# A four-layer FFN kernel on one core: its convolution kernel built in two halves, a fourth adapter buffer, and small steps of layers 2 and 3 in other places

## The reference

```
x = x + L0_ffn(L0_cond(x))   # long convolution along the features, masked; then a 512x512 FP8 weight
x = x + L1_ffn(L1_cond(x))   # one of 16 adapter matrices (512x512) per sequence; then SwiGLU, NF4 weights, hidden 1376
x = x + L2_ffn(L2_cond(x))   # 512x512 base + top-2 gated rank-16 experts; then 128 slots, top 8, uncertainty gate
x = x + L3_ffn(L3_cond(x))   # masked mean over features, 5-tap filter over tokens, sigmoid gate; 512x512 + rank-32 mix
```

## Time and profile before

| | us |
|---|---|
| median of 3 timed runs | 953.33 |
| lowest, highest | 950.3, 957.39 |
| the profiled execution, its own time | 951.24 |
| its span, first to last instruction | 949.5 |
| TensorE busy | 885.1 (93%) |
| VectorE busy | 579.8 (61%) |
| ScalarE busy | 390.1 (41%) |
| GpSimd busy | 86.9 (9%) |

### The profile page before, as it was taken

One profiled execution on the slowest core, in us unless ns is written; L12 is line 12 of the kernel. 1 busy time (PEld: TensorE's weight loads), 2 busy tenths in 40 slices (PEclk: granted clock), 3 DMA queues, 4 the chain that ended last, 5 costly groups with the idle time before them and its releaser, 6 DMA issues.

```text
span 949.5 us, 10316 instructions
## 1 busy us (share of the span) xinstructions
PE 885.1 (93%) x3261; PEld 474.5 (50%) x3262; DVE 579.8 (61%) x880; ACT 390.1 (41%) x458; POOL 86.9 (9%) x127
## 2 busy tenths in 40 slices
PE   0299998999999999999999999999989999899998
PEld 0296448998444444444444444444434555354442
DVE  7889977886998888888997300000132354158444
ACT  2024637876777776676687100000012132241200
POOL 5100009600000000000000000002201011100000
PEclk9999998999999999999999999999999999999999
DMA  6873127562000000000000300024010000002022
GB/s 203 317 242 134 74 81 246 195 223 70 23 22 23 17 31 0 31 30 1 30 1 0 87 13 1 0 72 136 1 45 1 1 1 1 1 1 44 0 89 88
DMA packets 32967, 61.19 MB, mean 64 GB/s; under 512 B 5880, under 2 KB 8264, under 8 KB 31704
## 3 DMA queue, kind: packets, MB, share of 16 engines
q1 hardware_dynamic: 32216, 60.50, 18.8%
q0 software_dynamic: 704, 0.10, 0.3%
HBM read 51.07 MB, written 8.47 MB: 63 GB/s over the span
## 4 chain that ended last, share of the span: by engine, by line
PE 83%; DVE 12%; issue 2%; DMA 1%; ACT 1%; POOLq 1%; POOL 0%; SPq 0%; ACTq 0%; DVEq 0%
PE ps L820 81%; DVE acc L1374 2%; DVE T L1374 2%; PE ps L861 1%; DVE W2T L1218 1%; PE ps L1075 1%; DVE W2T L1224 1%; POOLq L603 1%; DVE W2T L1221 1%; DVE raw L1352 0%; DVE amax L1345 0%; DMA T<-kpad 0%; DVE W1T L1218 0%; DVE Up L1551 0%; DVE Yp L1659 0%
## 5 line engine op out<-in xcount | busy, mean ns | idle before, releaser
L652 ACT ACTIVATE above<-raw,cst 128x1024 bf16<-128x1024 f32 (+2 forms) x225 | 271.8, 1231 | 122.1 <-DVE acc L1374 46.5
L820 PE MATMUL ps<-Yp,W3T 128*128 (+2 forms) x872 | 183.9, 367 | 6.6 <-POOL Yp L605 2.6
L1374 DVE SCALAR_TENSOR_TENSOR acc<-above,acc 128x1024 f32<-128x1024 bf16 (+2 forms) x112 | 148.1, 1323 | 18.3 <-ACT above L652 11.6
L820 PE MATMUL ps<-Up,W1T 128*128 128x512 f32 x344 | 155.5, 594 | 3.0 <-DVE Up L1473 1.9
L820 PE MATMUL ps<-Up,W2T 128*128 128x512 f32 (+1 forms) x392 | 155.1, 593 | 0.0
L820 PEld LDWEIGHTS ps<-Yp,W3T 128*128 128x128 f32 (+1 forms) x872 | 121.9, 196 | 63.7 <-issue 61.5
L1374 DVE SCALAR_TENSOR_TENSOR T<-above,T 128x1024 f32<-128x1024 bf16 (+1 forms) x84 | 114.1, 1359 | 20.9 <-ACT above L652 18.0
L820 PE MATMUL ps<-X,W3T 128*128 128x512 f32 (+1 forms) x256 | 113.7, 602 | 0.6 <-DVE Yp L1659 0.6
L820 PEld LDWEIGHTS ps<-Up,W2T 128*128 128x128 f32 (+1 forms) x392 | 64.2, 177 | 83.0 <-issue 83.0
L820 PEld LDWEIGHTS ps<-Up,W1T 128*128 128x128 f32 x344 | 64.1, 190 | 82.5 <-issue 76.3
L1495 DVE TENSOR_TENSOR X<-X,Yp x16 | 4.6, 349 | 125.6 <-issue 125.6
(11 more groups left out here) (299 smaller groups left out, 753.4 us busy)
## 6 DMA issues: line engine op xcount, KB each, us to landing
W3T<-in_wa SPq DMA_DIRECT2D x11, 1024.0 KB, 6.3
raw<-in_w SPq DMA_DIRECT2D x20, 256.0 KB, 3.3
W3T<-kpad SPq DMA_DIRECT2D x9, 512.0 KB, 5.0
Up<-in_xconv SPq DMA_DIRECT2D x4, 1024.0 KB, 11.5
X<-in_xT SPq DMA_DIRECT2D x1, 4096.0 KB, 22.9
xkeep<-X SPq DMA_DIRECT2D x4, 1024.0 KB, 4.5
X<-xkeep SPq DMA_DIRECT2D x4, 1024.0 KB, 9.6
W3T<-in_wa SPq DMA_DIRECT2D x5, 768.0 KB, 4.6
```

What stands on the lines that cost most here:

```text
L652: nc.scalar.activation(above[0:h, m % 2, 0:w], raw[0:h, u % 2, 0:w], ACT.Relu, scale=STEEP, bias=cst[0:h, C_BND + i:C_BND + i + 1]).then_i ...
L820: return nc.tensor.matmul(o, l, r, start=start, stop=stop, **kw)
L1374: V.scalar_tensor_tensor(out=ac, in0=src, scalar=float(STEPS[i]), in1=ac, op0=ALU.min, op1=ALU.add).then_inc(s["m_used"], 1)
```

## The change

- The convolution kernel is made in two halves of 16 heads: phases, sine, factors, matmuls and skip term each run twice with half the columns, into banks 6 and 7. The store to DRAM is four pieces per half. TensorE makes the second half after convolution group 1 (`make_k(1)`), and VectorE does `skip_term(1)` after `start_unit(0)`, ahead of the sort chain. SP stores the second half after strip 4.
- VectorE dequantises the FP8 weight after `conv_out(3)`; SP waits for that (`d_w0`) after issuing strip 8, then loads weight unit 1 and a quarter of X. X is loaded in quarters of 1 MB: two early, one after strip 8, one after strip 12.
- NCV, NF0, NAD become 4, 28, 54 instead of 10, 26, 50.
- Four adapter buffers: adapters 0 to 2 are loaded at the end of the convolution, 3 when the FFN ends, 4 right after; `keep(3)` and the load of unit 3 come behind adapter 4. GX and GA become 3; GpSimd copies the two further sequences. Unit 1 is transposed after the FFN, and copied by ScalarE after its three sequence copies.
- `prepare_values()`, the second part of `prepare()`, runs after the last down product.
- The four variance transposes of a block go to banks 3, 2, 5, 3.
- `slices(0)` is split in two and runs inside the last block of layer 2, one part before and one behind the wait for its `p_c2` inputs.
- Gates are spread in pairs: odd blocks lie in partitions 0 to 63, even ones in 64 to 127; a pair is two matmuls of 64 rows into banks 0 and 1. The memset of zeros on GpSimd goes.

```diff
-GX = 4
-GA = 4
+GX = 3
+GA = 3
...
-        NCV, NF0, NAD = 10, 26, 50
+        NCV, NF0, NAD = 4, 28, 54
@@ SP
             load_unit(0)
-            sp.dma_start(X[:, :, :], A["xT"].rearrange("(c p) n -> p c n", p=P)).then_inc(s["l_x"], 16)
+            load_x(0)
+            load_x(1)
...
-            sp.wait_ge(s["d_k"], 1)
-            for q in range(4):
-                sp.dma_start(kr[:, q * HQ:(q + 1) * HQ, :], ksb[q * 32:q * 32 + LA, :, :]).then_inc(s[f"l_kp{q}"], 16)
+            store_k(0)
...
                 if g == NS - 1:
+                    store_k(1)
+                if g == HG // 2:
                     sp.wait_ge(s["d_w0"], 1)
                     load_unit(1)
 
+                if g in (8, 12):
+                    load_x((8, 12).index(g) + 2)
...
             sp.wait_ge(s["p_conv"], HG)
-            load_adapter(0)
-            load_adapter(1)
+            sp.wait_ge(s["d_w0"], 1)
+            for a in range(NWS - 1):
+                load_adapter(a)
...
-            for a in range(2, ADAPT):
-                if a == 2:
+            for a in range(NWS - 1, ADAPT):
+                if a == NWS - 1:
                     sp.wait_ge(s["d_ord"], 1)
                     sp.wait_ge(s["p_ffn0"], TB * DC)
-                if a >= NWS:
-                    done = sp.value_load(order[0:1, NB + a - 2:NB + a - 1], min_val=0, max_val=NGR)
+                else:
+                    done = sp.value_load(order[0:1, NB + a - NWS + 1:NB + a - NWS + 2], min_val=0, max_val=NGR)
...
                 load_adapter(a)
-                if a == 2:
+                if a == NWS:
                     keep(TB - 1)
                     for u in units_between(K_FFN0[(TB - 1) * DC - 1], K_FFN0[-1]):
                         load_unit(u + 2)
@@ TensorE
                 last.then_inc(s["p_conv"], 1)
+                if g == 1:
+                    make_k(1)
...
                 for u in turns_ffn0(n):
-                    turn_unit(u)
+                    if u == 0:
+                        turn_unit(u)
...
+            turn_unit(1)
             pe.wait_ge(s["ad_out"], NG)
...
+            prepare_values()
             pe.wait_ge(s["d_x2"], NB // 2)
             pe.wait_ge(s["g_x2"], NB // 2)
...
                 if tb + 1 < TB:
                     logits(tb + 1)
+                else:
+                    pe.wait_ge(s["a_ha"], TB)
+                    slices(0, range(0, 2))
                 pe.wait_ge(s["d_hg"], tb + 1)
...
                     rank_in(tb + 1)
                     turn_logits(tb + 1)
+                else:
+                    slices(0, range(2, DC))
                 pe.wait_ge(s["a_c2"], tb + 1)
...
-                    if tb or t >= 2:
-                        pe.wait_ge(s["d_st"], NT * tb + t - 1)
-                    else:
-                        pe.wait_ge(s["a_va"], 1)
+                    if t == 0:
+                        pe.wait_ge(s["d_st"], NT * tb) if tb else pe.wait_ge(s["a_va"], 1)
+                    if t == 3:
+                        pe.wait_ge(s["d_st"], NT * tb + 1)
...
-                mm(ps[:, tb % 2, :], ones[:, :], gex[tb], True, True).then_inc(s["p_gb"], 1)
+                for k, half in ((0, slice(YM, P)), (1, slice(0, YM))):
+                    mm(ps[:, k, :], ones[half, :], gex[tb + k], True, True).then_inc(s["p_gb"], 1)
@@ VectorE
+            factors(0)
+            angles(1)
+            skip_term(0)
+            whole_turns(1)
...
+            factors(1)
...
             start_unit(0)
-            dve.wait_ge(s["l_w0"], 32)
-            link(V.tensor_copy(h16a, w0u))
...
+            skip_term(1)
             dve.wait_ge(s["p_ord"], 1)
...
                 conv_out(g)
-            dve.wait_ge(s["l_x"], 16)
+                if g == 3:
+                    dequantise_w0()
+                    dve.wait_ge(s["d_w0"], 1)
+            dve.wait_ge(s["l_x"], 16 * DC)
```

More of the change, by code:

```diff
@@ L286, in build @@
         mx2, gm2 = w2f[:, 4928:4930], w2f[:, 4932:4934]
-        gex = [w3f[:, i * TW:(i + 1) * TW] for i in range(TB)]
+        gex = [w3f[(0 if i % 2 else YM):(YM if i % 2 else P), i // 2 * TW:(i // 2 + 1) * TW] for i in range(TB)]
         wT = w3f[0:E, 2048:3072]
@@ L596, in _ @@
             g0 = GX + GA
-            first = [pool.value_load(order[0:1, g0 + i:g0 + i + 1], min_val=0, max_val=NB - 1) for i in range(12)]
+            first = [pool.value_load(order[0:1, g0 + i:g0 + i + 1], min_val=0, max_val=NB - 1) for i in range(14)]
             pool.wait_ge(s["d_x1"], TB * DC)
@@ L679, in _ @@
                                ).then_inc(s["a_xs"], 1)
+            evac_quant(1)
             for a in range(ADAPT):
@@ L820, in mm, with make_k @@
                 return nc.tensor.matmul(o, l, r, start=start, stop=stop, **kw)
-            pe.wait_ge(s["d_pp"], 1)
-            pe.wait_ge(s["d_kz"], 1)
-            for i in range(HQ):
-                for q in range(4):
-                    h = q * HQ + i
-                    last = mm(ps[q * 32:q * 32 + LA, 6, i * LC:(i + 1) * LC], pc[:, h, :], trig[:, h, 0:LC], True, True)
-            last.then_inc(s["p_k"], 1)
+            pe.wait_ge(s["d_kz"], 2)
+            def make_k(f):
+                pe.wait_ge(s["d_pp"], f + 1)
+                for i in range(HE):
+                    for q in range(4):
+                        h = f * HF + q * HE + i
+                        last = mm(ps[q * 32:q * 32 + LA, 6 + f, i * LC:(i + 1) * LC], pc[:, h, :], trig[:, h, 0:LC], True, True)
+                last.then_inc(s["p_k"], 1)
+            make_k(0)
             pe.wait_ge(s["l_cst"], 16)
@@ L970, in prepare, with prepare_values @@
                 last.then_inc(s["p_w16"], 1)
+            def prepare_values():
                 pe.wait_ge(s["a_v1"], 1)
@@ L1013, in turn_logits, with slices @@
                 nc.tensor.transpose(ps[:, 2, 0:P], lgT, ident).then_inc(s["p_lg"], 1)
+            def slices(tb, part=range(DC)):
+                if tb == 1:
+                    pe.wait_ge(s["a_q"], TB)
+                if tb == 2:
+                    pe.wait_ge(s["d_st"], TT)
+                pe.wait_ge(s["g_xc"], tb + 1)
+                for c in part:
+                    mm(ps[:, tb, :], wz[:, c, :], X[:, c, tok(tb)], c == 0, False)
             logits(0)
@@ L1074, in _ @@
                     for c in range(DC):
-                        last = nc.tensor.transpose(ps[:, 3 - t % 2, c * P:(c + 1) * P], Y[:, c, tile(tb, t)], ident)
+                        last = nc.tensor.transpose(ps[:, BANKS_ST[t], c * P:(c + 1) * P], Y[:, c, tile(tb, t)], ident)
                     last.then_inc(s["p_tr"], 1)
@@ L1086, in _ @@
                 last.then_inc(s["p_lr"], 1)
-            def slices(tb):
-                if tb == 0:
-                    pe.wait_ge(s["a_q"], TB)
-                if tb == 2:
-                    pe.wait_ge(s["d_st"], TT)
-                pe.wait_ge(s["g_xc"], tb + 1)
-                for c in range(DC):
-                    mm(ps[:, tb, :], wz[:, c, :], X[:, c, tok(tb)], c == 0, False)
             def slices_aux(tb):
@@ L1110, in turn_probs @@
                 last.then_inc(s["p_pt"], 1)
-            slices(0)
             slices(1)
@@ L1177, in _ @@
                 aux(n)
-            for tb in range(TB):
-                spread_gate(tb)
+            for tb in range(0, TB, 2):
+                spread_gates(tb)
             base(2)
@@ L1227, in _ @@
             V.memset(zpad, 0.0).then_inc(s["d_zp0"], 1)
-            V.memset(ps[:, 6, 0:HQ * LC], 0.0).then_inc(s["d_kz"], 1)
+            for f in range(2):
+                V.memset(ps[:, 6 + f, 0:HE * LC], 0.0).then_inc(s["d_kz"], 1)
             dve.wait_ge(s["l_s4"], 80)
```

139 lines of the change are left out of this document (83 added, 56 removed).

## The result

The changed kernel takes 957.98 us (median of 20 runs, 955.92 to 962.67), the kernel before 953.95 (20 runs, 950.3 to 957.64): a ratio of 1.0045, 95% interval 1.0029 to 1.0061. That is 4 us more, within the 1% that counts as none, where I had 1.4 less. It lies above the 950 that I gave and above the range, 943 to 956. A second measurement (run f0) gave 957.97 and again 1.0045 (1.0023 to 1.0067).

What follows compares the result with a forecast made beforehand. TensorE, holding 83% of the chain, was taken as the bound. Terms of +5.6 to the FFN's start, +2.4 in the adapters and -9.4 in layers 2 and 3 sum to -1.4 against 951.24; forecast 950 us, range 943 to 956.

Steps and rivals of the forecast that it cites:

- Head, two halves: Kernel start: halving the convolution kernel's making lets TensorE begin convolution group 0 5.0 us earlier.
- What the halves queue up: Convolution: strip 9 lands late behind the dequantised weight's wait; TensorE stands 8.5 us plus a 1.7 dip.
- Rival 1: Convolution: the strips do not stall, so the 8.5 us and the dip stay away: 940 us, chance 0.17.
- Adapters, what is removed: First adapter groups: transposes fill a gap, copies shrink, and the adapter 3 wait goes: -2.8 and -4.3 us.
- Layers 2 and 3: From before layer 2 on: values -3.7, three variance banks -2.5, slices -2.6, paired gates -0.6; sum -9.4 us.
- Rival 5: Layers 2 and 3: the tail gives nothing, dips stay and fills only move: 956 us, chance 0.05.
- rivals 2 and 3: Adapter stage does not stall, 940.5 us, chance 0.13; neither it nor the strips stall, 930 us, chance 0.10.
- I price each such dip at 1.7 us, and at nothing behind waits up to 2.0 us: TensorE's clock: a half-clock dip behind a longer wait costs 1.7 us, shorter waits cost no clock.
- with 1.2 us left no dip, -1.4: Before layer 2: with the gap mostly filled by value preparation, the clock stays up, gaining 1.4 us.
- What is added: Adapters: unit 3's late load delays VectorE and ScalarE's copies: +5.6 us with a dip, then +3.9 of further stalls.
- 0.7 at the first hidden product: End of the adapter stage: TensorE stalls 0.7 us at the first hidden product, part of the +3.9.
- Rival 4: Adapters: ScalarE's order holds VectorE up, ending the stage 12 us later: 962 to 965 us, chance 0.10.

Runs made afterwards that it cites:

- e1: Changed kernel with SyncE's wait for the dequantised weight and unit 1's load moved behind strip 12, later X quarters at groups 12 and 14: 948.02 us, ratio 0.9911.
- e7: Kernel before with four adapter buffers and their loads alone, counts 10, 26 and 50 kept: 948.62 us, ratio 0.9959.
- e4: Kernel before with the tail's edits alone (three variance banks, first slices inside layer 2, gates in pairs): 945.37 us, ratio 0.9906.
- e5: Kernel before with one edit alone, the values prepared behind layer 1's last down product: 950.56 us, ratio 0.9971.
- e2: Changed kernel with the load of raw unit 3 issued before adapter 3's weights, not behind them: 950.77 us, ratio 0.9963.
- e3: Changed kernel with both moves, the weight's wait with unit 1 later and unit 3's load before adapter 3's weights: 940.63 us, ratio 0.9836.
- e9: e3 with level counts 4, 30, 52 instead of 4, 28, 54: 937.21 us, ratio 0.9824.
- e13: e3 with level counts 4, 30, 48 instead of 4, 28, 54: 934.31 us, ratio 0.9795.
- e6: Kernel before with the head's edits alone (two halves, dequantisation moved, X in quarters, counts 4, 28, 54): 964.51 us, ratio 1.0117.
- e8: e3 with three unread 128x512 matmuls added behind the values' small ones, ahead of layer 2: 942.71 us, ratio 0.9892.
- e12: Kernel before with four adapter buffers, the values' move and the tail's edits, old head and counts: 938.91 us, ratio 0.9835.
- e14: e12 with level counts 10, 26, 46 instead of 10, 26, 50: 939.9 us, ratio 0.9845.
- f3: e3 measured once more, unchanged: 941.12 us, ratio 0.9857.
- e11: e3 with the values prepared in the last downs again and eight unread 128x512 matmuls before layer 2: 944.94 us, ratio 0.9901.

## Why the prediction was wrong

Right, by its own steps:
- *Head, two halves*: 5.0 foretold, 4.9 measured.
- *What the halves queue up*: `d_w0` at 62.6, measured 61.7; strip 9 at 70.3, measured 71.4; a stall of 8.5, measured 8.71 and 7.98 (f0). e1 shows the cause. Rival 1, that the strips do not stall, is out. Its doubt was right, though: the dequantisation took 5.2 us, not 6.7. Strip 9, behind 1.5 MB, was there 9.7 us after `d_w0`, not 7.7.
- *Adapters, what is removed*: the wait at adapter 3 is gone, and e7 gives 3.9 for the 4.3. Behind the 1.39 before the first group there was no half clock, as foretold.
- *Layers 2 and 3* without the values: 5.7 foretold (2.5 + 2.6 + 0.6), 5.8 between the traces from the first transpose of layer 2 on, 6.0 between the spans of before and e4. The timed 9.0 (6.1 to 11.8) is more than that; the runs' clocks had medians of 0.993 in e4 and 0.987 in before, so part of it is clock. Gates: 1.13 + 1.32 + 1.13 for 0.95 + 1.15 + 0.95. Rival 5 is out. With all stalls where I had them, rivals 2 and 3 are out as well.

Wrong are two steps, both too low. The first is the step that prices the clock, **"I price each such dip at 1.7 us, and at nothing behind waits up to 2.0 us"**. It took every stretch at half clock to be as long as those before, 3.4 us, and to need an idle time over 2 us ahead. The prediction's last line names this danger, "a clock that falls elsewhere", but its sum does not hold it. The change was to gain 1.4 us of clock; by the estimate above it lost 7.3 in the execution after and 2.1 in f0:
- Strip 9: 10.2 us at half clock, in which TensorE was busy for 6.0, so 3.0 lost instead of 1.7 (2.9 in f0).
- Adapters: 6.8 us, 3.0 lost instead of 1.7 (3.4 us in f0, 1.5 lost).
- Before layer 2, the step "with 1.2 us left no dip, -1.4": 6.8 us instead of none, so that logits and rank matmuls took 1.2 more than before where I had 1.4 less. e5 shows it alone.
- At 248.2, behind a wait of 2.8, and at 493.9: 1.7 each, in one execution of the two.

The second, as large or larger in the timed runs, is the term **"What is added"**. It foretold stalls of 3.9, 3.2 and 0.7 for the copies, 7.8; measured 10.6 and 11.1. Most of the difference is **"0.7 at the first hidden product"**: the wait there was 2.84 in both. It is as long in e1, e2 and e3, 1.45 in e9 and gone in e13, so it is the levels, and not the late unit. The first stall was 4.8 (5.3 in f0, in three pieces) for 3.9. Another 0.5 (1.0) of what the stage takes more than foretold is in no wait that I can name. The mechanism was right (unit 3 behind adapters 3 and 4 and `keep(3)`, VectorE waiting at level 35, ScalarE behind it: copy at 20.9 after the FFN for 20.4), and e2 takes 7.2 us out with it. Rival 4, which had ScalarE hold VectorE up for 12 us more, saw that levels set the stage's end, but its price is not found: the stage is 7 us longer in all.

The forecast also lost 2 us on its last line. The sum of -1.4 against the median before, 953.33, is 951.9; I wrote down the 2.1 between the profiled execution and the median and then gave 950. The 8.0 us between 950 and 957.98 are these 1.9, 0.6 by which the longer series has the kernel before higher, and 5.4, which are in the main the two steps.

On the order of the rings, which the prediction had from the Trainium skill (DMA: Bandwidth & Descriptors, Queues, rings and completion order): the strip, issued 0.5 us behind the quarter of X, landed 1.5 us after it, as the rule lets one expect, and e1, which issues the same bytes behind the strips, loses the stall.

## What to carry to other kernels

Move a wait on an issuing engine only with a list of everything queued behind it: here one wait in front of seven strips cost 10 us, and three transfers in front of a fourth 7, each mended by moving a few lines. When an early stage gets faster, ask which engine sets the end of the next one and deal its work out again, or the gain stops there. Give stalls on TensorE a second price for the clock, with its spread, from several executions, of the kernel before as well. When you take the clock out of a comparison, count only the half clock in which TensorE worked.

## What was not expected of the hardware

- Half-clock stretches came in lengths of 3.4, 6.8 and 10.2 us. The longest one, in all four executions with the strip's stall (after, f0, e2, e6), went on for 5.1 to 6.0 us after the matmuls had begun again (after: 71.5 to 77.5).
- The clock fell during dense matmuls with no idle time ahead, only small ones of 32 and 48 rows (e8), and an identical order lost it in some kernels and not in others. The same holds behind equal waits: after the 2.46 us near the adapters' first groups there was half clock in before, e4, e5, e6 and e7 and none in e12 and e14; after the 2.84 at the first up product there was in after, e1, e3, f3 and e11, and none in f0, e2 and e8.
- Two executions of one kernel differed by 5.5 us in span (960.9 and 955.4), 5.2 of it clock by the estimate above.
- The bit step of the dequantisation took 0.69 us in its new place (L1493), and 2.27 in the old one (L1395), where GpSimd was at work beside VectorE. The cast ahead of it took 1.23 there and 1.21 in the new place.
